# The node-row, edge and join work moved inside the counting stage of a four-layer graph kernel, one gather round for x rows and node numbers by destination, and one of four compares per tile moved from VectorE to GpSimd

## The reference

```python
edge_index = jnp.stack([src, dst])
x = _layernorm(x + _L0_gnn_ref(x, edge_index, edge_attr_17, ...))   # this layer is computed in prepare
x = _layernorm(x + _L1_gnn_ref(x, edge_index))                      # 10 propagation steps
x = _layernorm(x + _L2_gnn_ref(x, edge_index))                      # 16 propagation steps
x = _layernorm(x + _L3_gnn_ref(x, edge_index, ...))                 # two graph convolutions

def _L0_gnn_ref(x, edge_index, edge_attr, W1, b1, W2, b2, Ws, bs, Wn, bn):
    src, dst = (edge_index[0], edge_index[1])
    h = jax.nn.relu(edge_attr @ W1.T + b1)
    w = h @ W2.T + b2
    msg = w * x[src]
    agg = jax.ops.segment_sum(msg, dst, num_segments=x.shape[0])
    return jax.nn.relu(x @ Ws.T + bs + agg @ Wn.T + bn)
```

## Time and profile before

| what | us |
|---|---|
| median of the runs | 12517.22 |
| the profiled execution, own time | 12463.33 |
| its span | 12461.6 |
| mean granted TensorE clock | 0.548 of full speed |
| counting stage | 69.4 to 629.5 |
| node records | 629.5 to 655.6 |
| prepare, first to last instruction | 655.6 to 2623.2 |

### The profile page before, as it was taken

One profiled execution on the slowest core, in us unless ns is written; L12 is line 12 of the kernel. 1 busy time (PEld: TensorE's weight loads), 2 busy tenths in 40 slices (PEclk: granted clock), 3 DMA queues, 4 the chain that ended last, 5 costly groups with the idle time before them and its releaser, 6 DMA issues. The chain is left out here.

```text
span 12461.6 us, 88179 instructions
## 1 busy us (share of the span) xinstructions
PE 4407.2 (35%) x18774; PEld 3275.0 (26%) x18774; DVE 4688.8 (38%) x11607; ACT 3793.3 (30%) x11417; POOL 7372.8 (59%) x7464
## 2 busy tenths in 40 slices
PE   4610462343333333332033333333334332212533
PEld 3300352332222222221022222222222221111422
DVE  7900232233333333355034444444444443233333
ACT  3400462243222222226342222222223231134322
POOL 6767105426666667665656666666666666654455
PEclk8655555555555555555555555555555555555555
DMA  3211221133333333333123333333333333221211
GB/s 51 56 26 20 67 83 44 38 71 88 85 88 88 85 88 90 87 84 104 34 79 87 88 89 88 88 93 94 95 94 98 95 96 82 73 57 54 63 35 31
DMA packets 791320, 919.85 MB, mean 74 GB/s; under 512 B 258979, under 2 KB 676541, under 8 KB 790749
## 3 DMA queue, kind: packets, MB, share of 16 engines
q1 hardware_dynamic: 558638, 591.29, 15.5%
q0 software_dynamic: 232064, 323.36, 13.4%
q10 hardware_dynamic: 144, 0.10, 0.0%
HBM read 533.07 MB, written 388.06 MB: 74 GB/s over the span
## 5 line engine op out<-in xcount | busy, mean ns | idle before, releaser
L1624 POOL DMA_INDIRECT l_g<-tab,l x4704 | 4620.1, 982 | 2536.7 <-issue 1355.4
L1824 DVE TENSOR_TENSOR_SCAN l_w<-l_m,l_w,bank 96x512 f32<-96x512 bf16 x1248 | 1590.3, 1274 | 4350.1 <-remote 2797.1
L1661 PE MATMUL bank<-ident,l_w 96*128 96x96 f32 x5096 | 1092.0, 364 | 2537.9 <-DVE l_w L1824 2176.1
L1724 ACT ACTIVATE l_o<-l_o,coef_d 128x96 f32<-128x96 f32 x2940 | 857.1, 363 | 3162.2 <-DVE l_o L1852 1813.6
L1650 PE MATMUL bank<-ident,l_g 128*96 128x128 f32 x5096 | 1267.5, 399 | 1345.3 <-DMA l_g<-tab,l 602.5
L1661 PEld LDWEIGHTS bank<-ident,l_w 96*128 96x128 f32 x5096 | 846.5, 222 | 2833.4 <-DVE l_w L1824 2368.4
L1650 PEld LDWEIGHTS bank<-ident,l_g 128*96 128x96 f32 x5096 | 913.4, 190 | 1725.1 <-DMA l_g<-tab,l 640.4
L1720 ACT ACTIVATE l_o<-bank,coef_s 128x96 f32<-128x96 f32 x1764 | 450.4, 345 | 1809.7 <-remote 970.6
L278 PE MATMUL bank<-tail_up,v 96*96 96x500 f32 (+1 forms) x298 | 296.4, 1098 | 925.7 <-issue 660.4
L993 POOL DMA_INDIRECT XS<-in_x_dram,dst_i x196 | 198.0, 1010 | 710.7 <-DVEq L1337 647.3
L315 PE MATMUL bank<-ident,tail_up 96*125 96x96 f32 (+1 forms) x596 | 159.5, 423 | 867.8 <-issue 476.2
(11 more groups left out here) (292 smaller groups left out, 10764.1 us busy)
## 6 DMA issues: line engine op xcount, KB each, us to landing
tab<-l_o SPq DMA_DIRECT2D x1176, 192.0 KB
l_g<-tab,l POOLq DMA_INDIRECT x4704
l_m<-mask_d SPq DMA_DIRECT2D x784, 96.0 KB
l_m<-mask_s SPq DMA_DIRECT2D x490, 96.0 KB
x3t<-XS SPq DMA_DIRECT2D x98, 192.0 KB
prep_x<-in_x_dram SPq DMA_DIRECT2D x100, 187.5 KB
x1t<-prep_a SPq DMA_DIRECT2D x100, 187.5 KB
x3d<-prep_b SPq DMA_DIRECT2D x100, 187.5 KB
```

The lines of the kernel that those rows point to most:

```text
L1624: nc.gpsimd.indirect_dma_start(out=tile(G[q % RG], t), out_offset=None, in_=tables[0:table_at + (2 - p % 2) * TR, :] if p else first, in_o ...
L1661: last = nc.tensor.transpose(b_bank(q)[:, u * D:(u + 1) * D], W[q % RW][:, u:GE:U], self.ident[0:D, 0:D])
L1724: last = a.activation(tile(O[q % RO], t), tile(O[q % RO], t), ACT.Copy, scale=self.coef_d[:, t:t + 1])
L1824: v.tensor_tensor_scan(out=W[q % RW][:, :], data0=masks[q % RM][:, :], data1=a_bank(q)[0:D, :], initial=W[(q - 1) % RW][:, GE - 1:GE] if q ...
```

## The change

- The 100 row jobs and the 49 edge jobs stand inside the counting stage. An iteration `k` of it has two tiles and parts of a row job in several phases: PE transposes row job `k` and multiplies `k-1`, DVE adds and takes statistics of `k-2` and scales `k-3`, ACT normalises `k-4`, SP stores `k-5`. Edge jobs spread over the four tiles of a group. The loop is gone: the program of that stage is written out on every engine. Row jobs and edge jobs have one PSUM bank per step where they had two.
- The compare of the source's low digits (the first of the two L742) is POOL's, two tiles ahead (`low_digits`), and precedes `fine` in its program.
- In 25 pieces SP copies x (DRAM to DRAM) into a table `x_meta` with rows of 104 numbers; at the start of prepare one DMA writes the eight numbers of each of the 50000 nodes into the same table. POOL's rounds are now `meta` by source, `x_meta` by destination (104 numbers a row), and the record scatter: 588 instructions in place of 784.
- The edge records are made in two parts, 100 tiles before sum group 0 and 96 before sum group 12 (`HALF`, `FIRST`). The first needs 25 groups of the second round, the second all of it; POOL waits for each before it scatters that part.
- In the sum groups the products lag two groups behind the transposes in place of one, one semaphore (`stepped`) stands for PE's whole step, and SP stores group `g-5` after it has issued the mask of `g` (before, `g-3`).

```diff
@@ count_edges
+            self.XM = tmp("XM", [P, NT * (D + MF)])
+            row_turn, row_out, edge_in, edge_out = self.bank[4], self.bank[5], self.bank[6], self.bank[7]
...
-            def steps(eng, body):
-                body(0, 0)
-                with eng.Fori(0, (NI - 3) // 2) as k:
...
+                def low_digits(t):
+                    u = t % R4
+                    if t >= R4:
+                        pool.wait_ge(product, t - (R4 - 1))
+                        pool.wait_ge(fars, t - (R4 - 1))
+                    nc.gpsimd.tensor_scalar(ol[0][u][:, :], iota_lo[:, :], lo[0][:, t:t + 1], None, ALU.is_equal
+                                            ).then_inc(lows, 1)
...
+                for t in range(NT):
+                    if t + 2 < NT:
+                        low_digits(t + 2)
+                    pool.wait_ge(rounded, t + 1)
...
+                    if k % 4 == 1 and k // 4 < JOIN:
+                        some = slice(k // 4 * (N // JOIN), (k // 4 + 1) * (N // JOIN))
+                        sp.dma_start(self.both_t[some, 0:D], i["x"][some, :]).then_inc(R["joined"], 16)
...
+                for k in range(LAST):
+                    for t in (2 * k, 2 * k + 1):
+                        if t < NT:
+                            pairs(t)
+                            if t + 1 < NT:
+                                digits(t + 1)
+                        if 0 <= t - 2 < NT:
+                            tiles_before(t - 2)
+                        if t % U == 2 and t // U + 1 < NI:
+                            high_digits(t // U + 1)
+                        if t % 2 == 0:
+                            if 0 <= k - 2 < JN:
+                                rows(k - 2)
+                        else:
+                            if 0 <= k - 3 < JN:
+                                scale_rows(k - 3)
+                            if k % 2 and 0 <= (k - 3) // 2 < NI:
+                                gate((k - 3) // 2)
@@ prepare
-                for k, (index, of) in enumerate(((self.src_i, self.meta), (self.dst_i, self.meta), (self.dst_i, i["x"]))):
+                for k, (index, of, into) in enumerate(((self.src_i, self.meta, ms), (self.dst_i, self.both_t, rows_in))):
+                    if k:
+                        pool.wait_ge(S["joined"], 16)
...
+                    sp.dma_start(self.both_t[:, D:D + MF], self.meta[0:N, :]).then_inc(S["joined"], 16)
...
-                for k in range(2 * (NI + GATE)):
-                    if 0 < k <= JN:
-                        scale_rows(k - 1)
-                    if k < JN:
-                        rows(k)
...
+                for g in range(NGP + 3):
+                    if g in (0, FIRST):
+                        part = g // FIRST
+                        landed = NGP + (NGP if part else HALF)
+                        for q in range(landed - RG, landed):
+                            dve.wait_ge(self.fills(q), self.full(q))
+                        self.edge_records(dve, link, halves[part], part, ms, md, work[part], record, row, S)
+                        dve.sem_inc(S["made"], 1)
```

More of the change, by code:

```diff
@@ new lines, in _ @@
+                load(0)
+                for n in range(3):
+                    load_x(n)
+                sp.wait_ge(R["blank"], 1)
+                with nc.allow_non_contiguous_dma(reason="the attributes of four edges of each partition"):
+                    sp.dma_start(ea[:, 0:GF * U * ED].rearrange("p (g c) -> p g c", c=U * ED),
+                                 i["ea"][0:GF * GE, :].rearrange("(g p u) c -> p g (u c)", p=P, u=U)
+                                 ).then_inc(R["ea"], 16)
+                    sp.dma_start(ea[0:REST // U, GF * U * ED:NT * ED],
+                                 i["ea"][GF * GE:E, :].rearrange("(p u) c -> p (u c)", u=U)).then_inc(R["ea"], 16)
@@ new lines, in pairs, with tiles_before @@
+                def pairs(t):
+                    u, b = t % U, t // U % 2
+                    if t:
+                        dve.wait_ge(nears, t)
+                    v.scalar_tensor_tensor(
+                        out=junk_n[:, :], in0=sbr[:, b, u * P:(u + 1) * P], scalar=self.src_f[:, t:t + 1],
+                        in1=earlier[:, :], op0=ALU.is_equal, op1=ALU.mult, accum_out=near[:, t:t + 1]).then_inc(nears, 1)
+                def tiles_before(t):
+                    dve.wait_ge(looked, t + 1)
+                    if t:
+                        dve.wait_ge(fars, t)
+                    dve.wait_ge(lows, t + 1)
+                    v.scalar_tensor_tensor(
+                        out=junk_f[:, :], in0=look[t % 2], scalar=1.0, in1=ol[0][t % R4][:, :], op0=ALU.mult,
+                        op1=ALU.mult, accum_out=far[:, t:t + 1]).then_inc(fars, 1)
@@ new lines, in high_digits, with rows @@
+                def high_digits(n):
+                    b = n % 2
+                    dve.wait_ge(rows_in[b], 32 * (n // 2 + 1))
+                    for c in range(2):
+                        v.tensor_scalar(oht[:, b, c, :], hb[:, b, :], iota_p[:, c:c + 1], None, ALU.is_equal
+                                        ).then_inc(ohts, 1)
+                def rows(n):
+                    dve.wait_ge(R["product"], n + 1)
+                    x = X[n % XR][:, :]
+                    link(v.scalar_tensor_tensor(out=x, in0=row_out[0:NP_, 0:GD], scalar=0.0, in1=x, op0=ALU.max,
+                                                op1=ALU.add))
+                    dve.sem_inc(R["added"], 1)
+                    if n:
+                        dve.wait_ge(R["rooted"], n)
+                    if n >= SK:
+                        dve.wait_ge(R["normed"], n - SK + 1)
+                    for u in range(U):
+                        last = v.bn_stats(out=stat[:, u * 6:(u + 1) * 6], in_=x[:, u * D:(u + 1) * D])
+                    link(last)
+                    for u in range(U):
+                        last = v.bn_aggr(out=mv[:, u * 2:(u + 1) * 2], in_=stat[:, u * 6:(u + 1) * 6])
+                    link(last)
+                    link(v.tensor_single_scalar(mean[n % SK][:, :], mv[:, :].rearrange("p (u c) -> p u c", c=2)[:, :, 0],
+                                                -1.0, op=ALU.mult))
+                    dve.sem_inc(R["stats"], 1)
@@ new lines, in turn_edges, with hide, weigh @@
+                    last.then_inc(G["turned"], 1)
+                def hide(n):
+                    pe.wait_ge(G["copied"], n + 1)
+                    nc.tensor.matmul(edge_in[0:D, :], self.w1[:, :], eat[:, :], start=True, stop=True
+                                     ).then_inc(G["hidden"], 1)
+                def weigh(n):
+                    pe.wait_ge(G["rect"], n + 1)
+                    if n:
+                        pe.wait_ge(G["gated"], n)
+                    for u in range(U):
+                        last = nc.tensor.matmul(edge_out[:, u * D:(u + 1) * D], hid[:, u * P:(u + 1) * P], self.w2[:, :],
+                                                start=True, stop=True)
+                    last.then_inc(G["product"], 1)
@@ L808, in lookup @@
-                def lookup(t, u, b):
-                    pe.wait_ge(split.sem, split.at + t + 1)
-                    if not (isinstance(t, int) and t < 2):
-                        pe.wait_ge(fars.sem, fars.at + t - 1)
-                    k = 0
-                    for c in range(2):
-                        for part in (coarse, fine):
-                            last = nc.tensor.matmul(look[u % 2], oht[:, b, c, u * P:(u + 1) * P],
-                                                    part[u % 2][:, c * LO:(c + 1) * LO], start=k == 0, stop=k == 3)
-                            k += 1
-                    last.then_inc(looked.sem, 1)
```

718 lines of the change are left out of this document (336 added, 382 removed).

## The result

The changed kernel takes 11786.9 us (median of 4 runs, 11771.4 to 11810.6) against 12514.3 us before (12501.1 to 12523.0): a ratio of 0.942, 95% interval 0.940 to 0.944. It is 727 us faster; the forecast was 649 us, 11870 us. The profiled executions differ by 692 us (spans 12461.6 and 11769.3).

What follows compares the result with a forecast made beforehand. It took DVE to bound counting, and PE's held instruction rate the costliest stretches of prepare. Counting +329 us and prepare -978 us gave -649 us: 12517 to 11868, said as 11870 us, range 11690 to 12140.

Steps and rivals of the forecast that it cites:

- the time of a tile: Counting: 4.3 us for each of 196 tiles, 5% above PE's sum, plus 46 us around them, 889 us in all.
- rival 2: Counting: DVE's 3.7 us a tile bound it because busier PE keeps the higher clock; +211 us, 11750 us in all; 9%.
- The prediction's own sign: Counting in the new profile: about 890 us, with PE, not DVE, over 85% busy.
- rival 5: Counting: PE is held there too, making the kernel slower than before; at 8 us a tile +1054 us; 3%.
- The join: Start of prepare: the DMA joining `meta` into the table takes 55 to 188 us, hidden beside round one's 245 us.
- round one: Prepare: POOL's first gathers, 196 at 1.25 us each, 245 us.
- Round two: Prepare: POOL's second gathers, from 245 to 490 us after prepare's start.
- The first records: Prepare: DVE makes them after round two's 25th group, at 370 us, in 13 us; sum group 0 starts near 388.
- Held groups: Prepare: while POOL gathers without pause, PE passes one instruction per 1.40 us, so sum groups come 67.2 us apart.
- Rival 1: Counting: in-order programs pack badly, 6.0 us a tile; +662 us, 12201 us in all; 12%.
- rival 3: Prepare: the join is exposed, 131 us late at twice its upper price; 11990 us in all; 9%.
- Rival 4: Prepare: PE isn't held, so POOL's own chain decides, 750 us, -1218; 11628 us in all; 6%.

Runs made afterwards that it cites:

- compare_on_vector: The changed kernel with the low-digit compare of the sources back on VectorE: 11785.8 us, ratio to before 0.944.
- the last chip: Ran the changed kernel with 0.49 us pauses behind the first 41 groups' scatters and each gather group in the passes: 10569.9 us, 1.025 of before's 10313.4 there.
- three_rounds: The changed kernel without the joined table, prepare gathering in three rounds again: 12004.9 us, ratio to before 0.962.
- before_compare_on_gpsimd: The kernel before with only the low-digit compare of the sources moved to GpSimd, two tiles ahead: 12601.7 us, ratio to before 1.010.

## Why the prediction was right, and where it was off

**Counting, +329 us forecast, +185 measured.** The term that was off is the time of a tile: 4.3 us were taken, 3.61 measured (196 gathers from 82.7 to 786.8 us), which is 135 of the 144 us. Two of the sums below it were good: VectorE 3.63 against 667.1/196 = 3.40, and ScalarE 3.43 against 3.32. PE's was not: 4.08 against 606.9/196 = 3.10, with a clock of 0.78 as rival 2 had it. And 4.3 was built on PE's. The 5% above PE's sum that I chose belonged on the largest sum at the risen clock. Rival 2 put this at 3.7 us a tile; its counting half came true in the number, while that VectorE bounds the stage isn't shown. The prediction's own sign, PE over 85% busy and VectorE not, failed: PE is at 82% and VectorE at 90. PE wasn't held in counting (rival 5): between two gathers stand a compare and a difference of GpSimd.

**The moved compare.** I took 0.5 us, with 0.4 and 1.2 as ends; it is 0.963. It didn't bring the time down, as the prediction said, and compare_on_vector shows it: no difference in the node records' time. What VectorE gave up came back as longer instructions.

**The join** was hidden and took 36 us, under the forecast 55 to 188.

**Prepare, 990 us forecast.** From the node records' end (840.6) to the records' load it is 1047.8. The steps in order: round one 245, right. Round two 245 forecast, 276 measured: I took the pitch from one row of 0.95 + 0.30 us, while the grouped row of all 196, which I had not put beside it, says 1.40:

```profile
L993 POOL DMA_INDIRECT XS<-meta,dst_i x196 | 206.8, 1055 | 67.5 <-issue 67.5
```

(206.8 + 67.5)/196 = 1.40 us. Reading the single row cost 31 us here. The first records began at t = 387 instead of 370, by that pitch, and were made at 429 instead of 383: they took 42.4 us where 13 were forecast, because VectorE was held too, which the prediction had for PE alone. Held groups 67.2 us apart: exact. Second scatter at 736 instead of 662: 31 of the 74 us are the second round, 11 the first hundred scatters (1.40 us each, not 1.29), and 32 the way to group 12's gate and its records. The step under way when those scatters ended came in only 15 us after them, and the next 13.5 after that. The second scatter's end is at 859 instead of 786. In the held stretch behind it two steps, as forecast, and then free steps at 4.90 instead of 5.3 us, which gave 15 us back.

**The sum.** -978 became -920 and +329 became +185, errors of +58 and -144 us, which partly cancel, and that is luck; the passes' +42 takes part of it back, which leaves -43 us between forecast and profiled spans. On the medians the forecast stood 83 us over the measured time, inside its range. Rival 1 (6.0 us a tile) and rival 3 (the join exposed) failed. Rival 4 (PE isn't held) failed in the comparison, and is what the last chip shows in its second round.

**What stays open.** Of prepare's 920 us the round left out is worth 274 by three_rounds. The rest, the moved row and edge jobs and the records in two parts, is read from the traces; no run undoes it alone. Then, what the hold is. The runs show it beside GpSimd's indirect DMAs in an unbroken row, on PE's and on VectorE's instructions, at the same 1.40 us. They show that 0.49 us behind each DMA ends it for the sum groups but not, at first, for the records, and that a chip can be without it. They don't show by which path GpSimd's DMAs reach the other engines' instructions, nor what sets the chips apart, nor what the change is worth on a chip of the other kind. That the hold makes up all of the 17% between the chips isn't shown either. Its second round fits it. The passes are 871 us shorter there with the same code, and pauses on the other chips gave them 60 to 78. Either those pauses are too few or too short for the passes, or the chips differ in something else as well. A second round fed by SyncE's plain DMAs would have told issue from transfer; it wasn't run.

## What to carry to other kernels

Price a repeated instruction by its mean over all of its kind in the same regime, never by one row. Before moving work from VectorE to GpSimd, add a share of its GpSimd time to VectorE as well. It was 82 to 97% in the old counting stage and a third to a half in the new one, and in neither did the move win anything. When engines starve while GpSimd issues indirect DMAs back to back, try half a microsecond of something else behind each, and look at more than one chip before keeping it: such pauses were worth 1.4% on the chips with the hold. On one without it the kernel with pauses was 2.5% slower than before.

## What the runs showed of the hardware

- TensorE was let through at one instruction per 1.40 us beside unbroken indirect DMAs of GpSimd, whatever GpSimd's own pitch (1.40 in gathers, 1.29 in the last scatters; the groups stayed 67.3 us apart), in every profile of such DMAs but that of one chip.
- VectorE's instructions came 1.40 us apart too while it made the first records beside such gathers (42.4 us, and 17.1 us on the other chip).
- With the hold, gathers in the second round take 1.08 to 1.10 us, with pauses 0.95; on the other chip 0.94 without any.
- A 128x256 compare of bf16 takes 0.96 us on GpSimd and 0.28 us on an undisturbed VectorE, and it stretched VectorE by 82 to 97% of its length in the old counting stage, by a third to a half in the new one.
- In before_compare_on_gpsimd PE is 57% busy over the counting stage at a granted clock of 1.00 (2.4 GHz); before it was 60% busy at 0.68. Nothing in the experiment was meant to move the clock, and I don't know why it did.
- 50000 pieces of 32 bytes were joined into a table in 36 us.
